# Layer 0's attention heads: keys projected and roped before queries, key sums taken at the end of the list of the head before, first rope behind the first probabilities tile

## The reference, cut to what matters

```
x  = x + attn0(wkv(x, side, side), ...)      # then a top-1 mixture of experts
q, k, v = x@Wq, x@Wk, x@Wv ; g = sigmoid(x@Wg)
q, k = rope(q), rope(k)                      # t1*cos - t2*sin, t1*sin + t2*cos
k_cmp = mean of k over blocks of 64 tokens   # 8 blocks; v_cmp likewise
p_cmp = softmax(q.k_cmp, whole blocks of the past)
p_slc = softmax(q.k, causal)                 # top 8 of 8 blocks: all are taken
p_swa = softmax(q.k, causal and within 64 tokens)
o = g_cmp*(p_cmp@v_cmp) + g_slc*(p_slc@v) + g_swa*(p_swa@v)
x += concat(o over heads) @ Wo
```

## Time and profile before

| what | value |
|---|---|
| median of three runs | 2427.64 us |
| the profiled execution's own time | 2426.77 us |
| its span (first to last instruction) | 2425.1 us |
| PE busy | 2041.1 us (84%) |
| DVE busy | 1758.0 us (72%) |
| ACT busy | 1341.8 us (55%) |
| POOL busy | 1103.2 us (45%) |
| mean granted PE clock | 0.928 of full speed |
| layer 0's heads, about | 86 to 1300 us of the span |

### The profile page before, as it was taken

The page is one execution under the profiler, slowest core; times in us unless marked ns, Lnnn a source line. Parts: engine busy times, 40 slices in busy tenths (PEclk is TensorE's granted clock), DMA queues, the critical chain, the costliest instruction groups (busy, mean ns, idle before and its releaser), DMA issues. The chain is left out here.

```text
span 2425.1 us, 41851 instructions
## 1 busy us (share of the span) xinstructions
PE 2041.1 (84%) x14117; PEld 1254.2 (52%) x14117; DVE 1758.0 (72%) x3496; ACT 1341.8 (55%) x3199; POOL 1103.2 (45%) x758
## 2 busy tenths in 40 slices
PE   0578878999999999999995669966789899977999
PEld 0345545555565555555552635534556666553444
DVE  7788888888988888887773449954676778663770
ACT  4566656665666656655553424325675767546442
POOL 5675656665666565554442046643332222210440
PEclk9999988999999999999998579987888899879999
DMA  4232232222222221221212864455433333317110
GB/s 171 83 102 75 89 102 79 89 86 76 67 67 96 75 75 62 68 98 51 71 54 103 339 251 145 142 186 171 130 111 114 102 118 129 119 68 230 44 39 22
DMA packets 110015, 260.51 MB, mean 107 GB/s; under 512 B 10672, under 2 KB 39472, under 8 KB 107824
## 3 DMA queue, kind: packets, MB, share of 16 engines
q1 hardware_dynamic: 90320, 208.85, 25.6%
q10 hardware_dynamic: 16992, 41.43, 5.0%
q0 software_dynamic: 2560, 8.39, 1.0%
HBM read 179.46 MB, written 76.02 MB: 105 GB/s over the span
## 5 line engine op out<-in xcount | busy, mean ns | idle before, releaser
L824 PE MATMUL ps_q<-a_y,a_w 128*128 128x512 f16 x1536 | 342.9, 380 | 0.0
L619 POOL TENSOR_TENSOR a_rb<-a_rb,a_rot 128x512 f32<-128x512 f32 x129 | 189.1, 1466 | 291.7 <-ACT a_rb L730 291.2
L824 PEld LDWEIGHTS ps_q<-a_y,a_w 128*128 128x128 f16 x1536 | 148.4, 98 | 176.0 <-issue 1.3
L842 PE MATMUL ps_s<-a_kk,a_q 128*128 128x512 f32 (+3 forms) x512 | 190.7, 480 | 27.0 <-POOL a_kk L623 22.8
L270 DVE TENSOR_TENSOR_SCAN wkv_bwd<-wk_decay,wkv_tail,wkv_fwd 128x512 f32<-128x512 f32 x114 | 185.7, 1652 | 0.1
L831 PEld LDWEIGHTS ps_v<-a_w,a_y 128*128 128x128 f16 x3072 | 176.9, 98 | 15.1
L877 PE MATMUL ps_g<-a_o,a_wo 128*128 (+1 forms) x768 | 178.4, 382 | 7.3 <-POOL a_o L610 4.9
L831 PE MATMUL ps_v<-a_w,a_y 128*128 128x128 f16 x3072 | 182.0, 219 | 0.0
L866 PE MATMUL ps_o<-a_tt_,a_v 128*128 128x512 f32 (+3 forms) x512 | 168.5, 475 | 9.3 <-ACT a_tt_ L750 6.9
L966 DVE TENSOR_REDUCE a_nmax<-ps_s 128x1 f32<-128x512 f32 (+3 forms) x256 | 125.2, 489 | 64.6 <-PE ps_s L844 58.4
L1005 DVE SCALAR_TENSOR_TENSOR a_pt<-a_ewn,a_coef,a_pt 128x192 f32<-128x192 f32 (+1 forms) x256 | 168.2, 716 | 0.0
(11 more groups left out here) (281 smaller groups left out, 4928.0 us busy)
## 6 DMA issues: line engine op xcount, KB each, us to landing
a_w<-wqkv_split SPq DMA_DIRECT2D x48, 768.0 KB, 4.3
scratch_numlog<-wkv_nl ACTq DMA_DIRECT2D x40, 512.0 KB, 2.7
wkv_kt<-in_fT ACTq DMA_DIRECT2D x58, 256.0 KB, 2.7
a_wraw<-in_wqkv SPq DMA_DIRECT2D x18, 768.0 KB, 5.3
wqkv_split<-a_w SPq DMA_DIRECT2D x17, 768.0 KB, 6.8
a_stacks<-qk_parts SPq DMA_DIRECT2D x96, 128.0 KB, 2.6
gate_up<-in_gate_up SPq DMA_DIRECT2D x8, 1408.0 KB, 15.9
a_nlc<-scratch_numlog SPq DMA_DIRECT2D x18, 512.0 KB, 4.9
```

The lines of the kernel that those rows point to most:

```text
L619: pool.tensor_tensor(rb[:, n, :], rb[:, n, :], rot[:, 2 * n + 1, :], ALU.mult).then_inc(s["roped"], 1)
L824: mm = pe.matmul(psq[n][:], w16[:, i % 2, wp, n, c, :], y16[b % 2][:, yp, c, :], start=c + m == 0, stop=c == CC - 1 and m == 2)
L842: pe.matmul(cols(ps, j, -lead), q[:, j * P:(j + 1) * P], kk[:, NBLK - lead:NBLK + P * (j + 1)], start=True, stop=False)
```

## The change

Three edits, all in layer 0's attention.

1. The first projection is k and the second is q. The weights are stacked k, q, v instead of q, k, v, the cosine and sine tables change places with them, and POOL's two sums write kk first and q second. The number and shape of instructions stays.
2. `sum_keys` leaves its place ahead of the softmax of its own head. It is now the last thing that DVE does for the head before, right behind the window products, and it waits for the first rope half (k) only. One call ahead of the loop serves head 0. One call too many runs at the end, for a head 64 whose projection is only signalled, as the ropes of that head already were.
3. DVE's first rope of the next head leaves `between()` and stands behind the first of the four `pt` tiles (j = 3).

```diff
-        qk = (q[:], kk[:, NBLK:])
+        kq = (kk[:, NBLK:], q[:])
...
-                    pool.tensor_tensor(qk[n], ra[:, n, :], rb[:, n, :], ALU.add).then_inc(s["q_sb"], 1)
+                    pool.tensor_tensor(kq[n], ra[:, n, :], rb[:, n, :], ALU.add).then_inc(s["q_sb"], 1)
...
                 def sum_keys(g):
-                    dve.wait_ge(s["q_sb"], g * 2 + 2)
-                    dve.tensor_reduce(ksum, qk[1].rearrange("p (m n) -> p m n", n=BLK), AX,
+                    dve.wait_ge(s["q_sb"], g * 2 + 1)
+                    dve.tensor_reduce(ksum, kq[0].rearrange("p (m n) -> p m n", n=BLK), AX,
                                       ALU.add).then_inc(s["ksum"], 1)
...
                             op0=ALU.mult, op1=ALU.add).then_inc(s["p_step"], 1)
+                        if j == 3:
+                            rope(g + 1, 0)
                     rope(g + 1, 1)
...
-                        sum_keys(g)
                         if i == 2 and not final(b):
...
-                            rope(g + 1, 0)
...
                         softmax(b, g, c * G + i, between)
+                        sum_keys(g + 1)
...
                 rope(0, 0)
                 rope(0, 1)
+                sum_keys(0)
...
-    return np.ascontiguousarray(np.stack([cos * scale, sin * scale, cos, sin], 1) / np.float32(WSCALE).astype(np.float32))
+    return np.ascontiguousarray(np.stack([cos, sin, cos * scale, sin * scale], 1) / np.float32(WSCALE).astype(np.float32))
...
-    wqkv = np.stack([a["L0_attn_W" + x].reshape(CC, P, H0, D0) for x in "qkv"])
+    wqkv = np.stack([a["L0_attn_W" + x].reshape(CC, P, H0, D0) for x in "kqv"])
```

## The result

The changed kernel takes 2569.34 us, the median of four runs (2565.22 to 2571.26), against 2426.65 us for the kernel before, measured beside it. The ratio is 1.0593, with a 95% interval of 1.0569 to 1.0617: 5.9% slower. The forecast was 2608 us in a range of 2500 to 2650, slower with 0.91. The profiled execution's span is 2569.5 us, 144.4 us more than before.

The account below looks back on a forecast made before the run. PE's own list and the loop from maximum through probabilities, `values` and `scores` were taken to bound the kernel at nearly the same speed. Middle +120, last pass +60, first 0: +180 on 2426.77, forecast 2608 us, range 2500 to 2650.

Parts of the forecast that it names:

- The moved rope and POOL's four instructions: Middle heads: POOL's later rope instructions hold up the window products; probabilities complete 8.5 us behind the tiles' start, before 3.8.
- R: The end of the next head's first rope on DVE, the point from which the prediction counts times.
- my first rival: Only the k pair blocks the window products, done by R + 4.9: +88 us, 2515 us; chance 0.11.
- The head times: Four heads in a row, first maximum to first maximum: 86.4 us against 71.35, 15 us more per four heads.
- full blocking: All four window products held up by POOL's k and q pairs, probabilities complete at R + 7.2.
- The clock: PE behind a long gap runs at its lower clock level: `values` to `scores` 5.5 us instead of 3.55.
- my signs: What would show the forecast, such as middle window products at 4.5 to 6 us per head, PE's wait over 170 us.
- The key sums: On DVE behind the window products: no added wait while these are blocked, the same 0.6 us cost, PE later in most heads.
- k before q: No instruction more or less; q ready at R + 6.7, before PE comes to scores, so hidden.
- The first pass: The split stands behind the k pair instead of the q pair: between -45 and +43 us, taken as 0.
- The key sums' wait: Rival: no block, but DVE stalls for k ahead of the key sums: +56 us, 2483 us; chance 0.10.
- The faster one: Rival: the split leaves the first pass's window products, 4.7 to 1.9 us per head: 2382 us; chance 0.07.

Follow-up runs that it names:

- the small q pair: The changed kernel with POOL's product and sum of the second half (q) cut to 8 of 512 columns: 2483.39 us, ratio 1.0251.
- edit 3 alone: The kernel before with only DVE's first rope moved behind the first tile, q first and key sums as before: 2558.51 us, ratio 1.0541.
- the variants that made the k sum late: Changed kernel, POOL's first rope product waiting for complete probabilities: 2550.74 us; the moved split with window products ahead of the second rope: 2425.9 us.
- the moved split: The kernel before with POOL's weights' split of the first pass moved behind the second rope of that head: 2381.14 us, ratio 0.9846.

## Why the prediction was right, step by step

**The moved rope and POOL's four instructions: right.** R + 1.8 for the start of the products, R + 7.0 for the end (I had 1.85 and 7.2), one product per gap. The second product is recorded from 651.64, before POOL's k sum at 651.65, and still ends behind it, at 653.13:

```profile
651.64 1.49 DVE L1007 SCALAR_TENSOR_TENSOR a_pt<-a_ewn,a_coef,a_pt 128x192 f32<-128x192 f32 x1
```

Against the rule of the Trainium skill ("SBUF — State Buffer", "Who interferes with whom") read by its letter, two per gap, the trace decides once more: with four back-to-back POOL instructions four products end 0.15 us behind the last. The kernel with the small q pair shows it too: its products end at R + 4.9, the time that I gave my first rival, and not at the R + 4.3 that I had put beside it.

**The head times: right in shape, a quarter too large.** Forecast +180, measured +144.4 in the span. The middle heads took 83.7 us per four instead of my 86.4, and the middle passes 100 us more instead of 120. The last pass took 42 instead of 60: its heads grew by 11.6 us per four, and its last head, with none behind it, not at all. Of the 2.7 us per four heads that I had too much, 1.8 are in i = 3 and 0.7 in i = 1. Two terms were mis-sized, and a third, in i = 1, the other way (the clock, below).
- *i = 1*, start of the tiles: I took 8.16 us from the first maximum as unchanged. It is 7.15. Lines 989 and 992 also read two inputs from SBUF. Before, 989 met POOL's line 199 and 992 the q product, which the early rope had started; the kernel before, DVE and POOL:

```profile
616.28 1.01 DVE L989 TENSOR_TENSOR a_coef<-a_rsum,a_gate 128x12 f32<-128x12 f32 x1 [0.16 <-DVE a_rsum L987]
617.32 1.22 DVE L992 TENSOR_TENSOR a_pc<-a_ec,a_coef 128x32 f32<-128x32 f32 x1
```

```profile
616.00 1.26 POOL L199 TENSOR_TENSOR wkv_eukv<-wkv_euk,wkv_kt 128x512 f32<-128x512 f32 x1
617.22 1.27 POOL L619 TENSOR_TENSOR a_rb<-a_rb,a_rot 128x512 f32<-128x512 f32 x1
```

Now the first still costs 1.03 us (646.28, above), but the second meets nothing. The moved rope gave 1 us back here that I had not counted.
- *i = 3*, the products: I took full blocking, 5.2 us. Here it is 4.10, because ACT's list has the issue of a store between the two swaps, POOL waits 0.33 us for the second one, and two products slip through:

```profile
694.80 4.10 DVE L1007 SCALAR_TENSOR_TENSOR a_pt<-a_ewn,a_coef,a_pt 128x192 f32<-128x192 f32 x4
```

```profile
695.83 1.26 POOL L623 TENSOR_TENSOR a_kk<-a_ra,a_rb 128x512 f32<-128x512 f32 x1
697.42 1.34 POOL L619 TENSOR_TENSOR a_rb<-a_rb,a_rot 128x512 f32<-128x512 f32 x1 [0.33 <-ACT a_rb L730]
```

Heads with i = 0 (20.1 forecast, 20.1 measured on average) and i = 2 (20.3, 20.1) were right, the latter partly by luck: my 4.5 us from `values` to `scores` was the middle of two values, and single heads take 3.6 or 5.0 to 5.2, with a mean of 4.57.

**The clock: right, and a large part.** I had 5.5 us for `values` to `scores` behind a long gap. With i = 3 it was 5.38 (698.96 to 704.34), with i = 1 6.60, on average 5.29 and 6.12. The transposes take 2.4 us in both. In the head with i = 1 PE stays at its lower level until the matmuls with v are nearly done, and these take 4.41 us. The windows view, with 0.51 as the granted clock:

```profile
655.90:662.40 6.50, 6.50 (x18) 4.42 (x19) 4.93 (x7) 1.88 (x4) 0.00 (x0) 0.51 0.00 0
```

With i = 3 the level rises while they run, and they take 3.36 us. What the lower level costs in all can be estimated from the busy times: 41 of the 100 us in the middle passes. Of my signs one was missed: PE's wait for the probabilities is 163.1 us, not over 170.

**The key sums: the wait right, a queue missed.** They waited 1.6 us in the whole run, for head 0's k. But I followed only the scans behind them. In heads with i = 1 line 285 stands there too, ACT waits for it with line 695, and the copies of the transposed probabilities queue behind that on ACT:

```profile
657.04 0.63 ACT L695 ACTIVATE a_sg<-a_sg 128x512 f32<-128x512 f32 x1 [4.29 <-DVE a_sg L285]
```

This explains little of the 6.60: in the middle heads with i = 1 the matmuls with v begin 2.36 us behind the first transpose with all edits and 2.05 with edit 3 alone. Such heads take 22.7 us on average with all edits and 21.7 with edit 3 alone, and most of that 1 us is that the matmuls with v take 3.92 instead of 3.35 us. They are 0.45 us longer with i = 2 as well, where no line 285 stands. So the 10 us between the two kernels, whose intervals overlap, are mostly PE's clock; why it is lower with the key sums moved was not found.

**k before q: right** (0.9986, 1.0001). **The first pass: +3 against 0**, inside the bounds of -45 and +43: its window products fell from 75.21 to 70.28 us, and the time from `values` to `scores` grew by 2.9 us with i = 1 and 0.8 with i = 3.

**The rivals.** The k pair alone costs 60 us (2483.39 against 2423.28 beside it), where I had priced 88. The key sums' wait became large only in the variants that made the k sum late (185.1 and 115.5 us). The faster one had the right source, the split beside the products, and the wrong means: the change did not take the split away, the moved split did, for 42 us.

## What to carry to other kernels

A place on one engine's list can be good because of what another engine does in that moment. Before moving an instruction, follow it through the whole chain that it starts, and ask beside which instructions of the other engine the last link will run: here 0.6 us of DVE work moved by 3 us put four POOL instructions of 1.27 us upon four products of 0.33. Look for the same collision in the rest of the kernel: the one that was already there was worth 1.5%. Look also at what stands behind each link in its engine's list: here a late swap on ACT made the copies that PE waits for late. And taking away a wait for the first of two inputs brings nothing while the second comes last.

## What the runs showed of the hardware

The first section says that the engines meet only at semaphores; DVE and POOL meet in SBUF as well. A DVE instruction with both tensor inputs in SBUF makes no progress while a POOL instruction with SBUF inputs runs: a 0.33 us product took 3.12 us beside the split, and 1.1 to 1.5 us each beside rope instructions. POOL loses at most 0.11 us per instruction to these short products, and exactly one product passes per POOL instruction even where the gap between two POOL instructions is 0.14 us or none; with a gap of 0.33 us two pass. Beside the longer scans POOL loses as well, 2.74 and 2.00 us instead of 1.27. The key sums (0.69 us beside the split) and the tiles, which read one input from PSUM, are not held up.

A DVE instruction with one tensor input can be held up too. This TENSOR_SCALAR of the changed kernel takes 1.58 us beside a POOL product that starts 0.02 us behind it:

```profile
688.56 1.58 DVE L236 TENSOR_SCALAR wkv_euk<-wkv_ek_raw,wk_eu,wk_cap 128x512 f32<-128x512 f32 x1
```

```profile
688.58 1.27 POOL L195 TENSOR_TENSOR wkv_ekv<-wkv_ek,wkv_kt 128x512 f32<-128x512 f32 x1 [2.31 <-DVE wkv_ek L230]
```

In the kernel before it took 0.54 us where POOL started 0.16 us behind it, and POOL's product was the longer one:

```profile
614.37 0.54 DVE L236 TENSOR_SCALAR wkv_euk<-wkv_ek_raw,wk_eu,wk_cap 128x512 f32<-128x512 f32 x1
```

```profile
614.53 1.51 POOL L195 TENSOR_TENSOR wkv_ekv<-wkv_ek,wkv_kt 128x512 f32<-128x512 f32 x1 [2.16 <-DVE wkv_ek L230]
```

I had not expected how much of the price is PE's clock: behind a gap of 3.12 us ten transposes take 2.40 us instead of 1.25, and `values` to `scores` 6.60 us instead of 3.55.
